# The first mixture's 32 groups in parts of 8, 12, 8 and 4 in place of 4, 12, 12 and 4

## What is computed

```python
x = x + 0.5 * _L0_ffn_ref(_layernorm(x), ...)      # the first mixture ("gelu")
# inside:
logits = (x @ gate_w + gate_b) / TEMP               # 128 -> 8
masked = jnp.where(keep_top2, logits, -jnp.inf); gate_probs = softmax(masked)
h = gelu(einsum('bsd,edf->bsef', x, w1) + b1)       # 128 -> 512, per expert
expert_out = einsum('bsef,efd->bsed', h, w2) + b2   # 512 -> 128
out = einsum('bse,bsed->bsd', gate_probs, expert_out)
out = (out - mu) / sqrt(var + EPS) * ln_g + ln_b    # a norm behind the sum over experts
```

## Time and profile before

| | us |
|---|---|
| median of 3 runs | 1714.39 (1710.18 to 1715.52) |
| span of the profiled execution | 1697.2 |
| end of the first mixture's last `finish` | 373.6 |
| indirect DMAs of the first mixture, sends and fetches | 128 |

### The profile page before, as it was taken

The page is one execution under the profiler, slowest core; times in us unless marked ns, Lnnn a source line. Parts: engine busy times, 40 slices in busy tenths (PEclk is TensorE's granted clock), DMA queues, the critical chain, the costliest instruction groups (busy, mean ns, idle before and its releaser), DMA issues. The chain is left out here.

```text
span 1697.2 us, 28236 instructions
## 1 busy us (share of the span) xinstructions
PE 1114.7 (66%) x6835; PEld 926.2 (55%) x6836; DVE 765.2 (45%) x2839; ACT 553.5 (33%) x1653; POOL 751.0 (44%) x802
## 2 busy tenths in 40 slices
PE   2376888437656699867477548289799734768482
PEld 2375888434346588757376547234344334657372
DVE  5221324158671133544146313269979762335132
ACT  1133546247413255533032113134343301223131
POOL 3634263521054625545715552255645456442522
PEclk9787999678966799978688769589999955879696
DMA  8544567310023345544354436100000003445363
GB/s 251 169 143 138 183 197 245 109 41 1 0 81 111 130 165 196 181 133 139 109 198 159 140 118 205 53 0 1 1 0 0 0 29 127 165 152 203 117 208 106
DMA packets 198792, 199.71 MB, mean 118 GB/s; under 512 B 22212, under 2 KB 140310, under 8 KB 198678
## 3 DMA queue, kind: packets, MB, share of 16 engines
q1 hardware_dynamic: 123138, 136.22, 23.5%
q0 software_dynamic: 16384, 33.59, 6.6%
q10 hardware_dynamic: 59156, 28.57, 5.9%
HBM read 52.44 MB, written 49.02 MB: 60 GB/s over the span
## 5 line engine op out<-in xcount | busy, mean ns | idle before, releaser
L611 PE MATMUL gelu_hb<-gelu_xsT,gelu_weights 128*128 128x128 f32 x2208 | 340.1, 298 | 65.5 <-issue 61.3
L611 PEld LDWEIGHTS gelu_hb<-gelu_xsT,gelu_weights 128*128 128x128 f32 x2208 | 308.7, 213 | 75.4 <-issue 73.5
L708 ACT ACTIVATE gelu_hid<-gelu_hb,gelu_weights 128x128 f32<-128x128 f32 x736 | 208.8, 374 | 238.6 <-remote 127.1
L1190 POOL DMA_INDIRECT slots_x<-gelu_xn,gelu_index x176 | 172.4, 980 | 203.6 <-DVE gelu_index L921 154.2
L622 PE MATMUL gelu_ob<-w,gelu_hid 128*128 x1472 | 220.0, 292 | 43.8 <-issue 41.5
L961 DVE TENSOR_TENSOR gelu_ys<-gelu_ob,bias 128x128 f32<-128x128 f32 x184 | 51.7, 291 | 392.4 <-PE gelu_ob L622 176.1
L622 PEld LDWEIGHTS gelu_ob<-w,gelu_hid 128*128 128x128 f32 x1472 | 198.7, 206 | 51.4 <-issue 51.1
L611 PE MATMUL swiglu_hb<-swiglu_xsT,swiglu_weights 128*128 128x128 f32 x736 | 114.8, 302 | 27.3 <-issue 27.2
L611 PEld LDWEIGHTS swiglu_hb<-swiglu_xsT,swiglu_weights 128*128 128x128 f32 x736 | 104.2, 217 | 29.0 <-issue 29.0
L952 DVE TENSOR_TENSOR gelu_hid<-gelu_sil,gelu_hb 128x256 f32<-128x256 f32 x92 | 38.4, 419 | 151.9 <-ACT gelu_sil L712 82.0
L952 DVE TENSOR_TENSOR swiglu_hid<-swiglu_sil,swiglu_hb 128x256 f32<-128x256 f32 x92 | 38.5, 419 | 149.3 <-ACT swiglu_sil L712 72.8
(11 more groups left out here) (375 smaller groups left out, 1997.1 us busy)
## 6 DMA issues: line engine op xcount, KB each, us to landing
gelu_weights<-w SPq DMA_DIRECT2D x184, 258.0 KB
gelu_weights<-s SPq DMA_DIRECT2D x92, 256.0 KB
swiglu_weights<-s SPq DMA_DIRECT2D x92, 256.0 KB
gelu_xs<-slots_x SPq DMA_DIRECT2D x69, 256.0 KB
slots_y<-gelu_ys ACTq DMA_DIRECT2D x138, 128.0 KB
swiglu_xs<-slots_x SPq DMA_DIRECT2D x23, 256.0 KB
slots_y<-swiglu_ys ACTq DMA_DIRECT2D x46, 128.0 KB
slots_x<-zeros SPq DMA_DIRECT2D x2, 1984.0 KB
```

Of the source, the lines that this page charges most:

```text
L611: last = pe.matmul(hb[j][:, c * P:(c + 1) * P], weights[:, j, c * P:(c + 1) * P], xsT[j // SET][:, j % SET, :], start=True, stop=True)
L708: last = act.activation(hid[:, j % RING, c * P:(c + 1) * P], hb[j][:, c * P:(c + 1) * P], ACT.Gelu, bias=weights[:, j, FF + c:FF + c + 1])
L1190: pool.indirect_dma_start(slots_x[:, :], bass.IndirectOffsetOnAxis(index[p][:, k, g:g + 1], 0), tokens[p][:, g, :], None).then_inc(sent[p] ...
```

## The change

The first mixture's parts are 8, 12, 8 and 4 groups. The tables are moved to suit: part 0 now has two quads to send, fetch, scale, combine and finish, part 2 has two in place of three. The third quad of part 1 is scaled and combined in body 20, its finish comes behind the bodies. Other mixtures' tables are untouched.

```diff
-PARTS_OF = {("gelu",): ((4, 12, 12, 4),), ...
+PARTS_OF = {("gelu",): ((8, 12, 8, 4),), ...
@@ PE: beside
-   1: {0: at(turn_tokens, 2, 2), 2: at(logits, 2, 0) + at(logits, 2, 1) + at(logits, 2, 2)},
+   1: {2: at(logits, 2, 0) + at(logits, 2, 1)},
@@ ACT: beside
    12: {1: at(scale_lower, 0, 0)},
-   16: {1: at(scale_lower, 1, 0)},
...
+   13: {1: at(scale_lower, 0, 1)},
+   17: {1: at(scale_lower, 1, 0)},
+   18: {1: at(scale_lower, 1, 1)},
+   20: {1: at(scale_lower, 1, 2)},
@@ DVE: beside
-   16: {0: at(finish, 0, 0), 2: at(combine, 1, 0), 3: at(norm, 1, 0)},
...
+   16: {0: at(finish, 0, 0), 2: at(finish, 0, 1)},
+   17: {2: at(combine, 1, 0), 3: at(norm, 1, 0)},
...
+   20: {2: at(combine, 1, 2), 3: at(norm, 1, 2)},
+   21: {0: at(finish, 1, 0), 2: at(finish, 1, 1)},
@@ DVE: behind the bodies
-                combine(2, 2)
-                norm(2, 2)
+                finish(1, 2)
                 finish(2, 0)
                 combine(3, 0)
                 norm(3, 0)
                 finish(2, 1)
-                finish(2, 2)
@@ POOL
+            for q in range(QUADS[0]):
+                final_power(0, q)
             for q in range(QUADS[1]):
                 fetch(1, q)
-            for p in range(2):
-                for q in range(QUADS[p]):
-                    final_power(p, q)
...
             await_sets(-(-TILE0[3] // SET))
-            for q in range(QUADS[2]):
-                fetch(2, q, beside_products=q < QUADS[2] - 1)
+            final_power(1, 0)
+            final_power(1, 1)
+            fetch(2, 0)
+            final_power(1, 2)
+            fetch(2, 1, beside_products=False)
             final_power(2, 0)
...
-            for q in range(1, QUADS[2]):
-                final_power(2, q)
+            final_power(2, 1)
             final_power(3, 0)
```

More of the change, by code:

```diff
@@ L34 @@
 GROUPS = TOK // P
-PARTS_OF = {("gelu",): ((4, 12, 12, 4),), ("swiglu",): ((8, 12, 8, 4),), ("gelu", "swiglu"): ((4, 12, 8, 8), (8, 12, 8, 4))}
+PARTS_OF = {("gelu",): ((8, 12, 8, 4),), ("swiglu",): ((8, 12, 8, 4),), ("gelu", "swiglu"): ((4, 12, 8, 8), (8, 12, 8, 4))}
 PARTS = 4
@@ L761, in _ @@
             beside = {("gelu",): {0: {2: at(copy_tokens, 2, 0), 3: at(copy_tokens, 2, 1)},
-                                  1: {0: at(copy_tokens, 2, 2)},
                                   6: {0: at(copy_tokens, 3, 0)},
                                   12: {1: at(scale_lower, 0, 0)},
-                                  16: {1: at(scale_lower, 1, 0)},
-                                  17: {1: at(scale_lower, 1, 1)},
-                                  18: {1: at(scale_lower, 1, 2)},
+                                  13: {1: at(scale_lower, 0, 1)},
+                                  17: {1: at(scale_lower, 1, 0)},
+                                  18: {1: at(scale_lower, 1, 1)},
+                                  20: {1: at(scale_lower, 1, 2)},
                                   22: {1: at(scale_lower, 2, 0)}},
@@ L799, in _ @@
                 store(k, k % 2, len(kinds) - 1)
-            for p, q in {("gelu",): ((2, 1), (2, 2), (3, 0)), ("swiglu",): ((2, 0), (2, 1), (3, 0)),
+            for p, q in {("gelu",): ((2, 1), (3, 0)), ("swiglu",): ((2, 0), (2, 1), (3, 0)),
                          ("gelu", "swiglu"): ((6, 0), (6, 1), (7, 0))}[kinds]:
@@ L1068, in _ @@
                                   12: {2: at(combine, 0, 0), 3: at(norm, 0, 0)},
+                                  13: {2: at(combine, 0, 1), 3: at(norm, 0, 1)},
                                   14: {0: at(gates, 3)},
-                                  16: {0: at(finish, 0, 0), 2: at(combine, 1, 0), 3: at(norm, 1, 0)},
-                                  17: {0: at(finish, 1, 0), 2: at(combine, 1, 1), 3: at(norm, 1, 1)},
-                                  18: {0: at(finish, 1, 1), 2: at(combine, 1, 2), 3: at(norm, 1, 2)},
-                                  19: {0: at(finish, 1, 2)},
+                                  16: {0: at(finish, 0, 0), 2: at(finish, 0, 1)},
+                                  17: {2: at(combine, 1, 0), 3: at(norm, 1, 0)},
+                                  18: {2: at(combine, 1, 1), 3: at(norm, 1, 1)},
+                                  20: {2: at(combine, 1, 2), 3: at(norm, 1, 2)},
+                                  21: {0: at(finish, 1, 0), 2: at(finish, 1, 1)},
                                   22: {2: at(combine, 2, 0), 3: at(norm, 2, 0)}},
@@ L1129, in _ @@
             if later_weights:
-                beside[20] = {1: at(later_weights["spreads"], dve)}
+                beside[19] = {1: at(later_weights["spreads"], dve)}
             with_words = [p for p in range(1, min(NPARTS, PARTS + 1))] if gelu else []
```

## The result

| | median us | range, runs |
|---|---|---|
| before | 1713.48 | 1710.18 to 1715.52, 4 |
| changed | 1693.66 | 1692.29 to 1701.03, 4 |

Yet in the traces the last `finish` of the first mixture starts at 365.64 in place of 372.45, 6.8 earlier, nearly as forecast. The two don't fit, and the profiled execution's own time says in part why: with the change a span of 1692.2 belongs to a time of 1694.01. What lies around a span is 1.8 us, not 17.2. The profiled execution of before (span 1697.2) thus took about 1699.0, an estimate, 15 us less than the median it was set against. The two profiled executions are 5.0 us apart, the two medians 19.8.

A forecast was written before the change was run, and what follows sets the result against it. Engines stall beside POOL's bursts of indirect DMAs; between bursts the first mixture is bound by PE. Terms 4.5 - 11.8 + 12.2 - 11 - 1.1 = -7.2 took 1714.4 to 1707.2 us, range 1697 to 1720.

The forecast's parts named there:

- the runs' median is 17.2 above it, and I carry the difference over to 1714.39 unchanged: Whole kernel: terms priced on the profiled execution (span 1697.2) were added to the runs' median of 1714.39.
- Start: First mixture's first sends: `send(0)` has 16 DMAs in place of 8, so `send(1)` ends later, +4.5 us.
- with the same 24 DMAs, ends at 83.4: `send(1)` starts at about 52.0 in place of 47.44 and ends at 83.4 in place of 79: +4.5 us.
- Rival 1: Start costs all of the later first load, 9.5 us; sum -2.2, 1712.2 us, no change that shows; chance 0.20.
- My own sign of error, recovery later than 88: At the start: the forecast is wrong if the first body starts its recovery later than 88 us.
- `send(2)` and `fetch(0)`: `send(2)` falls from 24 to 16 DMAs, -11.8 us; `fetch(0)` grows from 8 to 16, +12.2 us.
- Clearing the slots: 512 KB of zeros move to the start, covered by `send(0)`: nothing; 1.6 us without that cover.
- `send(3)` and `fetch(1)`: Same counts and `shift`s, `fetch(1)` beside bodies 14 to 17 in place of 12 to 15: nothing.
- rival 4: `fetch(1)` beside the 256 KB loads costs 28.9 us in place of 13.3; sum +8.4, 1722.8 us; chance 0.10.
- `fetch(2)` and the end: `fetch(2)` falls from 24 to 16 DMAs, -11 us; DVE has 4 fewer operations before the last `finish`, -1.1.
- the list: Bursts with short pauses cost about 5.7, 17.9 and 29 us for 8, 16 and 24 indirect DMAs.
- Rival 3: Burst loss doesn't follow the DMA count, so only start and end are left: +3.4, 1717.8 us; chance 0.07.

The follow-up runs named there:

- one burst: Changed kernel with `final_power(1, 2)` put behind both eights of part 2's fetches, making one burst of 16: 1699.87 us, ratio 0.9963 to before.
- the fourth chip: Chip of the runs with long rests in single places and everywhere; bursts stall there, and the kernel before took 1685.47 us (1680.97 to 1693.19, 7).

## Why the prediction was right or wrong

The changed kernel came out below the range, and by the medians the gain was 19.8 us in place of 7.2. The terms can be held against seven traces of stalling chips: three of before (the one on record and two later; last `finish` starting at 372.45, 375.92, 376.28) and four of the change (365.64, 365.42 with one burst, 365.76, 359.44). Means in us, by the xs loads counted from the first and PE's turns; two of the traces of each are shown above:

| stretch | before | changed | difference | forecast |
|---|---|---|---|---|
| to the fifth load (start) | 104.2 | 110.3 | +6.1 | +4.5 |
| fifth to seventh load, `send(2)` | 45.3 | 32.7 | -12.6 | -11.8 |
| seventh to tenth, `fetch(0)` | 31.6 | 42.5 | +10.8 | +12.2 |
| tenth to fourteenth, `send(3)` | 39.8 | 37.2 | -2.6 | 0 |
| fourteenth to 21st, `fetch(1)` | 72.0 | 70.4 | -1.6 | 0 |
| 21st to the last `finish` | 82.0 | 71.0 | -11.0 | -12.1 |
| sum | 374.9 | 364.1 | -10.8 | -7.2 |

Two further traces, both from the fourth chip, have the old and the new parts up to `fetch(2)`, the new ones with rests in `send(0)`. They give -13.5, +11.9, -0.1 and -2.2 for the second to the fifth row.

**The step that failed** is "the runs' median is 17.2 above it, and I carry the difference over to 1714.39 unchanged". I took 17.2 for something that stands around every execution. Only 1.8 of it does; 15.4 are a difference between executions, and on two chips where bursts stall those of before went from 1696 to 1717 us. So the terms, read from one quick execution, were added to a median of others, and the range had no room for that. With the sum set against the profiled execution's own 1699.0, the forecast would have been 1691.8, and the changed kernel took 1693.66. That would have been luck: 1699.0 is no usual time of before (6 of 44 later ones on those two chips are below it), and 7.2 would have stayed far from the 19.8 between the medians.

Of that gap the sum itself explains 3.6: the traces give -10.8 where it has -7.2, above all because `send(3)` and `fetch(1)` stand at nought and came out at -4.2. The other 9 us stay open. The first comparison, four runs against four, gave -19.8, later ones -7.5 (with the power moved) and -11.9; the last agrees with the traces. The draw of the runs alone is a poor explanation, since all four times of before in the first comparison are 1710.18 or more, and only 10 of the 44 later ones are. The chip of the first comparison may have been slower for before or kinder to the change; no run shows it.

*Start*: the term was mis-sized, +6.1 in place of +4.5, and the first body's load is even 8.1 late (91.4 and 83.3 in the mean), though the old parts on the fourth chip have it at 67.8 and the fifth at 100.0, so it is not steady. The step "with the same 24 DMAs, ends at 83.4" took `send(1)` from 52.0; it starts at 58.0, since DVE is starved in `route(1)` beside the 16 unpaused DMAs of `send(0)`: with rests between them, and on the chip without stalls, that gap isn't there, and `send(1)` starts at 54.15 and at 51.5. I had noted such starving beside products and not applied it to the routing. That the late `send(1)` makes up the +1.6 is not shown, as `send(1)` 1.9 earlier left the fifth load where it was. Rival 1 is near for the first body (8.1 against 9.5), but not for the fifth load. My own sign of error, recovery later than 88, came true.

*`send(2)` and `fetch(0)`*: right, 0.8 and 1.4 us off. Together they are -1.8, as forecast near nought. *Clearing the slots* at nothing: no run contradicts it.

*`send(3)` and `fetch(1)`*: forecast 0. `fetch(1)` is right (-1.6, while traces of one kernel differ by up to 5.5), and rival 4, that it costs 28.9 beside the 256 KB loads, is refuted: the four bodies took 286.23 - 239.87 = 46.4, near the 45.2 of before. The stretch ahead gained 2.6; most is in one body, and I did not look into it. The two traces of the fourth chip don't have it (37.55 and 37.49), so it may be no effect of the parts.

*`fetch(2)` and the end*: -11.0 of -12.1. The turns alone are 24.9, 25.6, 24.0 and 23.9 apart, against 36.0, 36.1 and 35.3: -11.2 for the -11 of the forecast. Here the mechanism was right, too: on the stalling chips `fetch(3)` waits for the last store in both kernels, first before, then the change:

```profile
354.47 1.03 POOL L1199 DMA_INDIRECT gelu_back_small<-slots_y,gelu_index  x1 [2.94 <-DMA slots_y<-gelu_ys]
...
349.16 1.02 POOL L1199 DMA_INDIRECT gelu_back_small<-slots_y,gelu_index  x1 [2.94 <-DMA slots_y<-gelu_ys]
```

What the forecast did not see is that eight fetches fewer also gain on chips without stalls, there by POOL's chain. Nor is the count the whole price: the same 24 DMAs cost less when spaced wider, so the list holds for its short rests alone.

Rival 3, that the loss doesn't follow the count at all, falls: three terms of the list came out within 1.4 us. The Trainium skill ("Runtime: NRT & Kernel Launch", "Instruction fetch mechanics") says that the cost of crossing a block is mostly hidden. With 35.3 us between turns that are 249.20 - 240.74 = 8.5 apart where nothing stalls, the trace would disagree if these are late instructions, but that they are is only argued, from idle time that ends in "issue" on PE, DVE and ACT alike. The page of the profile counts as many instruction packets on a chip that stalls as on one that doesn't (48 and 66), so their number is not what differs.

## What to carry to other kernels

Before a sum is set against a median, compare the profiled execution's own time with it; a gap wider than what lies around the span is spread between executions. It belongs into the range, and a few more runs of the unchanged kernel, on more than one chip, are worth more than a finer term. Where engines idle on "issue" beside a run of indirect DMAs, try wider spaces between them before rearranging who waits for what: four short awaited operations per four DMAs gave 6.5% on the old parts here, and 8% in all bursts together with the change; the rearrangement gave 0.4 to 1%. Judge it by the end of the last products or of the stage, not by the one body beside the burst, because the wider burst moved part of its stall into the next body here: of 24 us won between two turns, 14 were left behind the products. Try it on more than one chip, because where nothing stalls the spaces cost a little (4 to 5 us in a mixture of 295).

## What was unexpected of the hardware

- The same program took 1685 to 1713 us in four of the comparisons and 1337 and 1333 in two, each on a chip of its own as far as is known. The difference shows beside POOL's bursts: same DMA durations (0.96 us), same bytes, but beside `send(2)` PE is busy 23.96 of 24.4 us on the one sort and 11.62 of 31.5 on the other. Why chips differ is open.
- The stall reaches PE, ACT and DVE, the last also on a chain of tiny operations: DVE needed 11.4 us for what takes 2.
- The granted clock falls with it: 0.68 in the window beside `fetch(2)`, 1.00 beside a burst that doesn't stall.
